# Later gates and additions behind the last scores, and an undivided last output projection, in a gated cross-attention block

## The chip, the cores and the metric

The kernel runs on 1 core of one Trainium2 chip. The metric is the device time of one execution in microseconds (us). The core has engines that run side by side, each through its own instructions in order: TensorE (PE in the profile, with its weight loads as PEld), VectorE (DVE), ScalarE (ACT), GpSimd (POOL) and SyncE (SP), which here issues the transfers. An engine waits for another by a semaphore: the instruction that needs a value waits until the counter has reached it, and everything behind it on that engine waits too.

## The reference

The block is a gated cross-attention followed by a gated mixture layer (4 batches, 256 rows, width 512, context of 1601 rows, 32 query heads over 8 key-value heads of 128):

```python
x = x + tanh(g_xattn) * attention(layernorm(x), ctx)      # q, k, v with biases, softmax, @ Wo + bo
# attention, for each head:
scores = q @ k.T / sqrt(128);  attn = softmax(scores);  o = attn @ v      # v holds the bias bkv
x = x + tanh(g_ffn) * ffn(layernorm(x))
# ffn:
base = h @ base_W.T
w = weights of the two likeliest of 8 experts, softmax(h @ router_W.T)
out = base + 2 * ((h @ lora_A) * w) @ lora_B
```

All of it is float32. For precision most products are made of three: each operand is cut into an upper and a lower part (names that end in `h` and `l`), and the lines of `three` multiply low by high, high by high and high by low.

## The kernel before

**Units and slots.** The attention is cut into 64 units (`UN`; a batch and two heads, 512 columns of q), and each unit into 13 score tiles of up to 128 context rows (`NT`), so there are 832 tiles (`TN`). All engines walk through the same list of slots `s`. In slot `s` TensorE makes the scores of tile `s` into `psS` (two banks, by turns); ScalarE copies them to `xs`; VectorE keeps a running maximum `mrun`. When a unit is done, job `m` turns the maximum, job `b` spreads it over the lanes (`mb` on ScalarE), GpSimd takes it off the scores (L798). In slot `s` ScalarE makes the two exponentials of tile `s - 17` (L988 to `psP`, two banks, for most tiles; L991 to `ph`, a ring of four), VectorE makes the lower part `pl` (L1046) and adds the tile to the unit's sum `psum_` (L1302). The first three tiles of a unit have their sums and lower parts made by GpSimd (L802, L807, and L813, which merges them into the unit before). In slot `s` TensorE multiplies tile `s - 19` by the values (L609 to L611; called PV below, and PV(62, 8) is that of tile 8 of unit 62). The upper part of a tile's exponential may be written only when PV of the tile four before it is done.

**The end of a unit.** Job `s` turns the unit's sum, VectorE reduces it and takes the reciprocal (L1207, L1209), job `r` spreads it (L476), ScalarE copies it to `rbc`, VectorE multiplies the PV result by it (`divide`, L1244), ScalarE makes `oh` with the value bias (L952), VectorE makes `ol` (L1247), and jobs `o0` and `o1` multiply by the output weights (`proj_o`). VectorE adds the product into `acc` (`add_o`, L1085). The last unit, 63, is the last work of the attention.

**The mixture layer.** It runs over 8 row tiles of `x` (0 to 5 from the batches already done, in `x1`; 6 and 7 in `acc`, which need the last unit). `ht` turns the normed tile, `mi` multiplies by the inner weights, the routing on VectorE is four pieces (`route_off`, `route_first`, `route_second`, `route_weights`; the last scales `mid`), `ga` turns the scaled inner tile (L505) for ScalarE to copy (`ffn_gated`), `ya` and `yb` are the two halves of the base product (L519), `yl` adds the last product (`ffn_lora`, L523), and `ffn_out` (L1129) on VectorE adds the result to the tile, after which it is stored. The products of tiles 0 to 5 use the two banks of `psS` by turns, so `ya2` waits until `ffn_out` of tile 0 has run (semaphore `s_yc`), `ya3` for tile 1, and so on.

**What sets the order.** Nothing but the code: a table of names by slot (`names_of` for every unit, and a second table behind it with slots counted from `TN`, the first slot without scores) says which job stands in which slot. TensorE, ScalarE and SyncE act on a job in its slot, VectorE one slot later, behind the running maximum and ahead of the lower part and sum of that slot. PE takes the four banks of `psW` in turn, each when the one that used it before has been read (`take`, `emptied`).

## Time and profile before

| | us |
|---|---|
| median of 3 runs | 2326.78 |
| lowest, highest | 2322.87, 2327.78 |
| the profiled execution | 2328.26 |
| its span in the profile | 2326.4 |
| TensorE busy | 2263.9 (97%) |
| VectorE busy | 1812.9 (78%) |
| ScalarE busy | 1664.8 (72%) |
| GpSimd busy | 1629.7 (70%) |

The profile is one execution; its instructions have a start, a duration and, from the semaphores, the instruction that ended each wait. The last scores are made at 2250 us of the span, and everything that the change touches but two instructions of one column, at slots 26 and 27, lies behind that. A time such as 2277.63 below is a moment of the span in us.

### The profile page before, as it was taken

What the parts mean: (1) busy time and instruction counts of PE and PEld (TensorE: products, weight loads), DVE (VectorE), ACT (ScalarE), POOL (GpSimd) and SP (SyncE); (2) the same over time, 40 slices, a digit from 0 to 9 for tenths busy, and PEclk for the clock granted to TensorE, in tenths of its full rate; (3) what the DMA queues carried; (4) which work ended last, traced back from release to release, by engine and by line L of the source; (5) the groups of instructions that cost most, each with busy time, mean ns of one, the idle gap of its engine ahead of it and who ended that gap; (6) DMA issues with size and microseconds to landing.
All of it is one profiled execution on the core that took longest, in us unless ns stands there. A gap on an engine that the chain in (4) does not pass through costs nothing.

```text
span 2326.4 us, 37328 instructions
## 1 busy us (share of the span) xinstructions
PE 2263.9 (97%) x12333; PEld 1942.2 (83%) x12333; DVE 1812.9 (78%) x3162; ACT 1664.8 (72%) x3149; POOL 1629.7 (70%) x1372
## 2 busy tenths in 40 slices
PE   6999999999999999999999999999999999999998
PEld 6888888888878888888888888888788888888865
DVE  5888888888777787777778778787777778778675
ACT  4777777777767777776777777777777777777663
POOL 5887887967657777856757777875766756766762
PEclk9999999999999999999999999999999999999989
DMA  7344344554333342325214343333423223222211
GB/s 257 132 153 136 128 149 135 159 198 141 98 104 123 112 145 91 125 98 184 91 60 151 97 136 123 110 113 105 168 78 100 91 70 108 64 96 82 87 51 55
DMA packets 139583, 273.69 MB, mean 118 GB/s; under 512 B 22785, under 2 KB 56065, under 8 KB 139137
## 3 DMA queue, kind: packets, MB, share of 16 engines
q1 hardware_dynamic: 122400, 255.71, 32.5%
q10 hardware_dynamic: 16992, 15.59, 2.9%
q8 instruction: 100, 1.64, 0.3%
q14 instruction: 91, 0.74, 0.1%
HBM read 204.27 MB, written 66.98 MB: 117 GB/s over the span
## 4 chain that ended last, share of the span: by engine, by line
PE 77%; DVE 10%; issue 4%; ACT 3%; POOL 3%; DMA 3%; ACTq 0%; DVEq 0%; SPq 0%; POOLq 0%
PE psW L412 11%; PE psW L413 11%; PE psW L414 11%; PE psS L412 6%; PE psS L414 6%; PE psS L413 6%; PE psW L609 6%; PE psW L611 6%; PE psW L610 6%; DVE psum_ L1302 3%; PE psW L468 3%; DVE mrun L1267 3%; POOL xs L798 2%; DMA rbc<-scr_r 1%; PE psW L476 1%
## 5 line engine op out<-in xcount | busy, mean ns | idle before, releaser
L798 POOL TENSOR_TENSOR xs<-xs,mb 128x512 f32<-128x512 f32 (+1 forms) x832 | 1064.5, 1305 | 514.6 <-ACT mb L869 514.5
L1267 DVE TENSOR_TENSOR mrun<-psS,mrun 128x512 f32<-128x512 f32 (+1 forms) x704 | 481.6, 684 | 338.2 <-ACT xs L869 337.2
L869 ACT ACTIVATE xs<-psS 128x512 f32<-128x512 f32 (+1 forms) x832 | 496.9, 597 | 241.2 <-PE psS L414 229.5
L1046 DVE TENSOR_TENSOR pl<-psP,ph 128x512 fp32r<-128x512 f32 (+1 forms) x672 | 458.8, 683 | 93.5 <-ACT ph L991 88.3
L991 ACT ACTIVATE ph<-xs 128x512 fp32r<-128x512 f32 (+1 forms) x832 | 518.6, 623 | 0.1
L1302 DVE TENSOR_TENSOR psum_<-psP,psum_ 128x512 f32<-128x512 f32 (+1 forms) x672 | 456.0, 679 | 0.8 <-POOL pl L802 0.8
L988 ACT ACTIVATE psP<-xs 128x512 f32<-128x512 f32 (+1 forms) x672 | 400.9, 597 | 39.5 <-DVE rinv L1209 14.9
L412 PE MATMUL psS<-ql,kh 128*128 128x512 f32 (+1 forms) x832 | 340.7, 409 | 20.1 <-DVE mrun L1267 18.9
L609 PE MATMUL psW<-ph,vh 128*128 128x512 f32 (+1 forms) x832 | 335.5, 403 | 10.4 <-DVE pl L1046 7.5
L611 PE MATMUL psW<-ph,vl 128*128 128x512 f32 (+1 forms) x832 | 329.2, 396 | 0.0
L610 PE MATMUL psW<-pl,vh 128*128 128x512 f32 (+1 forms) x832 | 328.9, 395 | 0.0
L413 PE MATMUL psS<-qh,kh 128*128 128x512 f32 (+1 forms) x832 | 328.8, 395 | 0.0
L414 PE MATMUL psS<-qh,kl 128*128 128x512 f32 (+1 forms) x832 | 328.7, 395 | 0.0
L412 PE MATMUL psW<-wvl,ch 128*128 128x256 f32 (+1 forms) x832 | 239.7, 288 | 0.0
L413 PE MATMUL psW<-wvh,ch 128*128 128x256 f32 (+1 forms) x832 | 234.5, 282 | 0.0
L414 PE MATMUL psW<-wvh,cl 128*128 128x256 f32 (+1 forms) x832 | 233.8, 281 | 0.0
L609 PEld LDWEIGHTS psW<-ph,vh 128*128 128x128 f32 (+1 forms) x832 | 156.7, 188 | 59.7 <-DVE pl L1046 14.0
L611 PEld LDWEIGHTS psW<-ph,vl 128*128 128x128 f32 (+1 forms) x832 | 156.8, 188 | 37.7
L412 PEld LDWEIGHTS psS<-ql,kh 128*128 128x128 f32 (+1 forms) x832 | 154.5, 186 | 40.3 <-ACT xs L869 16.7
L610 PEld LDWEIGHTS psW<-pl,vh 128*128 128x128 f32 (+1 forms) x832 | 157.4, 189 | 36.3 <-issue 1.9
L414 PEld LDWEIGHTS psS<-qh,kl 128*128 128x128 f32 (+1 forms) x832 | 153.4, 184 | 39.0 <-issue 0.6
L412 PE MATMUL psW<-cl,wkh 128*128 128x384 f32 (+1 forms) x512 | 178.1, 348 | 4.4 <-DVE cl L1046 4.4
(188 smaller groups left out, 4396.5 us busy)
## 6 DMA issues: line engine op xcount, KB each, us to landing
wqh<-scr_wq SPq DMA_DIRECT2D x96, 256.0 KB, 2.6
wql<-scr_wq SPq DMA_DIRECT2D x96, 256.0 KB, 3.0
woh<-scr_wo SPq DMA_DIRECT2D x48, 512.0 KB, 3.2
wol<-scr_wo SPq DMA_DIRECT2D x48, 512.0 KB, 4.2
rbc<-scr_r ACTq DMA_DIRECT2D x59, 256.0 KB, 3.4
scr_wq<-wqh SPq DMA_DIRECT2D x32, 256.0 KB, 2.3
scr_wq<-wql SPq DMA_DIRECT2D x32, 256.0 KB, 2.8
scr_wo<-woh SPq DMA_DIRECT2D x16, 512.0 KB, 3.4
```

The source lines that it names most:

```text
L412: eng.matmul(o, lh, rl, start=first, stop=False)
L413: eng.matmul(o, lh, rh, start=False, stop=False)
L414: return eng.matmul(o, ll, rh, start=False, stop=last)
L609: eng.matmul(o, vh[0:rows, t, hs], hi, start=t == 0, stop=False)
L610: eng.matmul(o, vh[0:rows, t, hs], lo, start=False, stop=False)
L611: eng.matmul(o, vl[0:rows, t, hs], hi, start=False, stop=t == NT - 1).then_inc(s_pv)
L798: eng.tensor_tensor(tile, tile, mb[0:rows_of(t), U % 2, :], ALU.subtract).then_inc(s_sub)
L869: return eng.activation(hi, src, ACT.Copy)
L991: eng.activation(ph[0:rows, T % RP, :], xs[0:rows, T % RX, :], ACT.Exp).then_inc(s_h)
L1046: return eng.tensor_tensor(lo, src, f32(hi), ALU.subtract)
L1267: eng.tensor_tensor(run, psS[0:rows, s % 2, :], a, ALU.max).then_inc(s_m)
L1302: eng.tensor_tensor(total, p, total, ALU.add).then_inc(s_a)
```

## The change

There are two parts.

**The table of the last slots.** The gates `ga0` to `ga5` move from slots 1 to 3 behind the last scores to slots 5 to 8; `yl0` and `yl1` stand together in slot 6, `ya1` and `yb1` come up to slots 2 and 3, and `yb3`, `yl3` and `ya4` move to slot 22. The second half of the routing and the scaling of `mid` (`route_second`, `route_weights`) move on VectorE from the end of slot `TN - 1` and the front of slot `TN` to the end of slot `TN + 3`. A new rule `goes_later` puts `ffn_out` and the additions of unit 62 two slots behind their product, at the end of the slot on VectorE, instead of one slot behind it and ahead of that slot's sums.

**The last unit.** Unit 63 is not divided. ScalarE takes the upper part straight from the PV result, VectorE the lower part, with no value bias. The value bias's own product (`c`, `proj_bias`) is made of a two-part cut of the bias (`bvh`, `bvl`, cut once at slots 26 and 27) times the output weights, 6 products. The four head-and-row-tile products stand apart (`proj_o_apart`), two in `psP` and two in `psW`. VectorE then adds the bias product to both tiles of `acc` (times tanh of the gate), and each of the four products times the reciprocal sums and the gate (`rtg`): 6 additions where there were 2. The turn of the reciprocal (`r`), its copy, and the division are gone, and job `s` of unit 63 stands one slot earlier, ahead of PV(63, 12).

```diff
 
-        return 9 if sum_by_mem(V) else 8
+        return 9 if sum_by_mem(V) else 8 if V < UN - 1 else 6
 
...
         names_of = {0: "k1 - k2 v0 q0 k3 q1 v1 - v2 - v3 -", UN: "- - - - - s - r - - o0 - o1",
-                    UN + 1: "- - - - - s - r - - o0 o1",
+                    UN + 1: "- - - - s c o0 o1",
                     UN - 1: "m - b - p1 s - r - - o0 - -"}.get(U, (AT_MEM if U >= 2 and sum_by_mem(U - 2) else AT)[U % 4])
...
     for s, names in {-15: "ht0", -13: "ht1 mi0", -12: "ht2 mi1", -11: "ht3 mi2", -10: "ht4 mi3", -9: "ht5",
-                     -8: "mi4", -7: "mi5 rt0", -1: "m", 0: "b o ya0", 1: "yb0 ga0 ga1", 2: "yl0 ga2 ga3",
-                     3: "ya1 ga4 ga5", 4: "yb1", 6: "yl1", 8: "ya2", 9: "yb2", 11: "yl2",
-                     14: "ya3", 16: "yb3", 17: "yl3", 21: "ya4"}.items():
+                     -8: "mi4", -7: "mi5 rt0", -1: "m", 0: "b o ya0", 1: "yb0", 2: "ya1", 3: "yb1", 5: "ga0 ga1", 6: "yl0 yl1 ga2 ga3",
+                     8: "ga4 ga5 ya2", 9: "yb2", 11: "yl2", 14: "ya3", 22: "yb3 yl3 ya4"}.items():
         for name in names.split():
...
 
+        def apart(t, h):
+
+            return bank_of(("o", UN - 1, 2 + h)) if t else psP[:, h, :]
+
         def gates_of(i):
...
 
+            def proj_o_apart(t):
+
+                have_weight("o", UN - 1, NU)
+                pe.wait_ge(s_ol, UN)
+                for h in range(2):
+                    if t:
+                        take(("o", UN - 1, 2 + h))
+                    cs = slice(h * 256 + t * 128, h * 256 + (t + 1) * 128)
+                    three(apart(t, h), oh[:, cs], ol[:, cs], woh[:, h, :], wol[:, h, :]).then_inc(s_o)
+                    if t:
+                        emptied(("o", UN - 1, 2 + h), s_acd, 2 * UN + 2 * t + h + 1)
+
+            def proj_bias():
+
+                have_weight("o", UN - 1, NU)
+                pe.wait_ge(s_bvl, 1)
+                o = take(("c", UN - 1, 0))
+                for h in range(2):
+                    m = three(o, bvh[:, 0:1].to_broadcast([128, 128]), bvl[:, 0:1].to_broadcast([128, 128]),
+                              woh[:, h, :], wol[:, h, :], h == 0, h == 1)
+                m.then_inc(s_vb)
+                emptied(("c", UN - 1, 0), s_acd, 2 * UN)
+
             def ffn_mid(i):
...
                     emptied(("pv", s // NT - 2, 0), s_ol, s // NT - 1)
-                if s == TN + 1:
+                if s == TN + 5:
                     emptied(("rt", 0, 0), s_wt, 6)
...
                 u = V % NU
-                act.wait_ge(s_on, V + 1)
+                if V == UN - 1:
+                    act.wait_ge(s_pv, NT * UN)
+                else:
+                    act.wait_ge(s_on, V + 1)
                 if V:
                     act.wait_ge(s_o, 2 * V)
+                if V == UN - 1:
+                    upper(oh[:, :], bank_of(("pv", V, 0))).then_inc(s_oh)
+                    return
                 eng.activation(oh[:, :], bank_of(("pv", V, 0)), ACT.Identity, bias=bkv_sb[:, 8 + u // 2:9 + u // 2]).then_inc(s_oh)
...
                     root(2, 2, NQ)
+                if s == 26:
+                    upper(bvh[:, :], bkv_sb[:, 15:16]).then_inc(s_bvh)
                 if s == NT * (UN - 7) - 1:
...
 
+                if V == UN - 1:
+                    if step == 0:
+                        dve.wait_ge(s_oh, UN)
+                        lower(ol[:, :], bank_of(("pv", V, 0)), oh[:, :]).then_inc(s_ol)
+                    return
                 if step == 0:
...
 
+            def goes_later(kind, n, part):
+
+                return kind == "yl" or kind == "o" and n == UN - 2
+
             def running_max(s):
...
                 for j in jobs.get(s - 1, []):
-                    if (j[0] not in "ms" or not TN - NT < s <= TN) and not goes_first(*j):
+                    if (j[0] not in "ms" or not TN - NT < s <= TN) and not goes_first(*j) and not goes_later(*j):
                         after_job(*j)
-                if s == TN:
-                    route_weights(1)
                 T = s - EXP
...
                         eng.tensor_tensor(total, pair_of(UT)[:, 0, :], total, ALU.add).then_inc(s_a)
+                for j in jobs.get(s - 2, []):
+                    if goes_later(*j):
+                        after_job(*j)
                 if TN - NT <= s < TN:
...
                     floored_var(2, NQ)
+                if s == 27:
+                    dve.wait_ge(s_bvh, 1)
+                    lower(bvl[:, :], bkv_sb[:, 15:16], bvh[:, :]).then_inc(s_bvl)
                 if s == 26:
...
                     route_first(1)
-                if s == TN - 1:
+                if s == TN + 3:
                     route_second(1)
-            add_o(UN - 1, 0)
-            dve.wait_ge(s_acd, 2 * UN - 1)
-            stats(6, tile_of(6))
-            add_o(UN - 1, 1)
-            dve.wait_ge(s_acd, 2 * UN)
-            stats(7, tile_of(7))
+                    route_weights(1)
+            dve.wait_ge(s_r, UN)
+            settle(eng.tensor_scalar(rtg[:, :], rinv[:, (UN - 1) % 2, :], tg[:, 0:1], None, ALU.mult))
+            dve.wait_ge(s_vb, 1)
+            for t in range(2):
+                dve.wait_ge(s_acd, 2 * UN - 2)
+                eng.scalar_tensor_tensor(acc[:, t, :], bank_of(("c", UN - 1, 0)), tg[:, 0:1], acc[:, t, :],
+                                         ALU.mult, ALU.add).then_inc(s_acd)
+            for t in range(2):
+                for h in range(2):
+                    dve.wait_ge(s_o, 2 * UN - 2 + 2 * t + h + 1)
+                    dve.wait_ge(s_acd, 2 * UN - 1 + t if h == 0 else 2 * UN + 2 * t + 1)
+                    eng.scalar_tensor_tensor(acc[:, t, :], apart(t, h), rtg[:, 2 * h + t:2 * h + t + 1], acc[:, t, :],
+                                             ALU.mult, ALU.add).then_inc(s_acd)
+                dve.wait_ge(s_acd, 2 * UN + 2 * t + 2)
+                stats(6 + t, tile_of(6 + t))
             floored_var(6, 8)```

Where its instructions stand. The order is fixed when the program is built. Names are those of the buffers; `[waits ...]` are the semaphores.

TensorE, from the first base product behind the last scores to the base product of tile 2, `ya2` (the row that waits for `s_yc`; left out are most rows of the PVs and of the base products, and repeats). Before, the gates (`mid`) of tiles 0 and 1 stand first of all and the reciprocal (`rinv`) last:

```order
L505 MATMUL psW<-ident,mid 128x128 [waits s_mb,s_wt]
L505 MATMUL psW<-ident,mid 128x128 [waits s_acd,s_wt]
...
L523 MATMUL psS<-lb_sb,midT 128x512 [waits s_gc]
L505 MATMUL psW<-ident,mid 128x128 [waits s_wt]
...
L505 MATMUL psW<-ident,mid 128x128 [waits s_gc] x2
...
L468 MATMUL psW<-ident,psum_ 128x128 [waits s_gc,s_ap]
...
L523 MATMUL psS<-lb_sb,midT 128x512
...
L476 MATMUL psW<-ident,rinv 128x128 [waits s_gc,s_r]
...
L609 MATMUL psW<-ph,vh 128x512 [waits s_lp]
...
L519 MATMUL psS<-bw_sb,hT 128x512 [waits s_yc]
```

```order
L477 MATMUL psW<-ident,psum_ 128x128 [waits s_mb,s_ap]
...
L537 MATMUL psW<-ident,mid 128x128 [waits s_acd,s_wt]
L537 MATMUL psW<-ident,mid 128x128 [waits s_wt]
L645 MATMUL psW<-ph,vh 128x512 [waits s_lp,s_r]
...
L555 MATMUL psS<-lb_sb,midT 128x512 [waits s_gc] x2
L537 MATMUL psW<-ident,mid 128x128 x2
...
L485 MATMUL psW<-ident,rinv 128x128 [waits s_gc]
...
L537 MATMUL psW<-ident,mid 128x128 [waits s_gc]
L537 MATMUL psW<-ident,mid 128x128 [waits s_rb]
L551 MATMUL psS<-bw_sb,hT 128x512 [waits s_yc]
```

The turn of the sum of unit 62 (`psum_`) now stands ahead of all gates, PV(63, 0) waits for the reciprocal (`s_r`), and both first `yl` stand together behind it.

VectorE, from the reciprocal of unit 62 to its `ol` (`x<-psS` is `ffn_out`; the first `pl` is that of tile 3 of unit 63, the second that of tile 4):

```order
L1209 RECIPROCAL rinv<-ssum 128x4 [waits s_d]
L1129 SCALAR_TENSOR_TENSOR x<-psS,tg,x 128x512 [waits s_y]
L1046 TENSOR_TENSOR pl<-psP,ph 128x512 [waits s_h]
L1302 TENSOR_TENSOR psum_<-psP,psum_ 128x512 [waits s_lp]
L1244 TENSOR_TENSOR psW<-psW,rbc 128x512 [waits s_rb,s_pv]
L1046 TENSOR_TENSOR pl<-psP,ph 128x512 [waits s_h]
L1302 TENSOR_TENSOR psum_<-psP,psum_ 128x512 [waits s_a]
L1247 SCALAR_TENSOR_TENSOR ol<-psW,bkv_sb,oh 128x512 [waits s_oh]
```

```order
L1253 RECIPROCAL rinv<-ssum 128x4 [waits s_d]
L1090 TENSOR_TENSOR pl<-psP,ph 128x512 [waits s_h]
L1353 TENSOR_TENSOR psum_<-psP,psum_ 128x512 [waits s_lp]
L1293 TENSOR_TENSOR psW<-psW,rbc 128x512 [waits s_rb,s_pv]
L1090 TENSOR_TENSOR pl<-psP,ph 128x512 [waits s_h]
L1353 TENSOR_TENSOR psum_<-psP,psum_ 128x512 [waits s_a]
L1173 SCALAR_TENSOR_TENSOR x<-psS,tg,x 128x512 [waits s_y] x2
L1296 SCALAR_TENSOR_TENSOR ol<-psW,bkv_sb,oh 128x512 [waits s_oh]
```

Before, `ffn_out` of tile 0 stood four rows above the first row shown, and that of tile 1 is the second row here; now both stand behind tile 4 of unit 63.

VectorE at the end, from the last unit's sum to its last statistics:

```order
L1207 TENSOR_REDUCE ssum<-psW 128x4 [waits s_rt,s_su]
L1209 RECIPROCAL rinv<-ssum 128x4 [waits s_d]
L1244 TENSOR_TENSOR psW<-psW,rbc 128x512 [waits s_rb,s_pv]
L1247 SCALAR_TENSOR_TENSOR ol<-psW,bkv_sb,oh 128x512 [waits s_oh]
L1085 SCALAR_TENSOR_TENSOR acc<-psW,tg,acc 128x512 [waits s_acd,s_o]
L1090 BN_STATS steps<-acc 128x6 [waits s_acd]
L1092 BN_AGGR mv<-steps 128x2 [waits s_bs]
L1085 SCALAR_TENSOR_TENSOR acc<-psW,tg,acc 128x512 [waits s_o,s_d]
L1090 BN_STATS steps<-acc 128x6 [waits s_acd]
```

```order
L1253 RECIPROCAL rinv<-ssum 128x4 [waits s_d]
L1090 TENSOR_TENSOR ol<-psW,oh 128x512 [waits s_oh]
L1173 SCALAR_TENSOR_TENSOR x<-psS,tg,x 128x512 [waits s_y]
L1401 TENSOR_SCALAR rtg<-rinv,tg 128x4 [waits s_r]
L1405 SCALAR_TENSOR_TENSOR acc<-psW,tg,acc 128x512 [waits s_acd,s_vb,s_d]
L1405 SCALAR_TENSOR_TENSOR acc<-psW,tg,acc 128x512
L1411 SCALAR_TENSOR_TENSOR acc<-psP,rtg,acc 128x512 [waits s_acd,s_o] x2
L1134 BN_STATS steps<-acc 128x6 [waits s_acd]
L1136 BN_AGGR mv<-steps 128x2 [waits s_bs]
L1411 SCALAR_TENSOR_TENSOR acc<-psW,rtg,acc 128x512 [waits s_o,s_d]
L1411 SCALAR_TENSOR_TENSOR acc<-psW,rtg,acc 128x512 [waits s_acd,s_o]
L1134 BN_STATS steps<-acc 128x6 [waits s_acd]
```

`ffn_out` of tile 3 (`x<-psS`) now stands between the last `ol` and the six additions.

## Rows read from the trace of the kernel before

**Rows 1.** The page: the span, TensorE's busy time, and the chain that ended last.

```profile
span 2326.4 us, 37328 instructions
...
PE 2263.9 (97%) x12333; PEld 1942.2 (83%) x12333; DVE 1812.9 (78%) x3162; ACT 1664.8 (72%) x3149; POOL 1629.7 (70%) x1372
...
PE 77%; DVE 10%; issue 4%; ACT 3%; POOL 3%; DMA 3%; ACTq 0%; DVEq 0%; SPq 0%; POOLq 0%
```

**Rows 2.** Stretches behind the last scores: length, busy by engine, granted clock, DMA.

```profile
2250.40:2257.00 6.60, 4.08 (x17) 2.92 (x16) 6.23 (x14) 3.31 (x7) 1.30 (x2) 0.76 0.00 0
2257.00:2261.00 4.00, 4.00 (x10) 2.64 (x10) 3.73 (x16) 1.63 (x3) 3.15 (x3) 0.54 0.11 18
2261.00:2271.00 10.00, 10.00 (x36) 5.76 (x34) 5.15 (x9) 5.17 (x14) 6.04 (x6) 1.00 0.25 98
...
2301.20:2312.00 10.80, 10.74 (x36) 6.12 (x36) 5.92 (x16) 1.07 (x3) 0.00 (x0) 1.00 0.07 25
```

**Rows 3.** ScalarE's timeline: start, duration, line, tiles; in brackets the wait.

```profile
2258.19 0.62 ACT L991 ACTIVATE ph<-xs 128x512 fp32r<-128x512 f32 x1
...
2264.52 0.45 ACT L869 ACTIVATE midT<-psW 128x128 f32<-128x128 f32 x2 [5.71 <-PE psW L505]
...
2272.88 0.62 ACT L991 ACTIVATE ph<-xs 128x512 fp32r<-128x512 f32 x1
```

**Rows 4.** VectorE's timeline behind the last scores.

```profile
2256.30 0.21 DVE L1163 TENSOR_TENSOR psW<-psW,rs 128x48 f32<-128x48 f32 x1
...
2258.65 1.27 DVE L1178 TENSOR_TENSOR mid<-mid,psW 128x128 f32<-128x128 f32 x6
...
2267.24 0.74 DVE L1129 SCALAR_TENSOR_TENSOR x<-psS,tg,x 128x512 f32<-128x512 f32 x1
...
2272.58 0.69 DVE L1207 TENSOR_REDUCE ssum<-psW 128x4 f32<-128x512 f32 x1 [3.37 <-PE psW L468]
```

**Rows 5.** GpSimd's timeline: the merge of unit 62's sum.

```profile
2269.29 1.28 POOL L813 TENSOR_TENSOR psum_<-pp,psum_ 128x512 f32<-128x512 f32 x1 [3.96 <-DVE psum_ L1302]
```

**Rows 6.** TensorE's timeline: behind the last scores, and at the last unit's end.

```profile
2262.49 1.88 PE L519 MATMUL psS<-bw_sb,hT 128*128 128x512 f32 x4
...
2274.37 0.50 PE L609 MATMUL psW<-ph,vh 128*128 128x512 f32 x1 [0.27 <-POOL pl L802]
...
2276.83 0.50 PE L609 MATMUL psW<-ph,vh 128*128 128x512 f32 x1 [1.06 <-POOL pl L802]
...
2277.63 1.88 PE L519 MATMUL psS<-bw_sb,hT 128*128 128x512 f32 x4
...
2297.50 0.65 PE L476 MATMUL psW<-ident,rinv 128*128 128x128 f32 x4 [1.00 <-DVE rinv L1209]
...
2301.20 0.47 PE L412 MATMUL psW<-wol,oh 128*128 128x512 f32 x1 [1.32 <-issue]
...
2310.05 1.02 PE L523 MATMUL psS<-lb_sb,cst 128*128 128x512 f32 x2
2310.91 0.60 PE L468 MATMUL psW<-ident,hn 128*128 128x128 f32 x4
```

**Rows 7.** VectorE's timeline at the end.

```profile
2302.86 0.75 DVE L1085 SCALAR_TENSOR_TENSOR acc<-psW,tg,acc 128x512 f32<-128x512 f32 x1 [1.76 <-PE psW L414]
...
2305.37 0.69 DVE L1090 BATCH_NORM_STATS2 steps<-acc 128x6 f32<-128x512 f32 x1
...
2307.75 0.55 DVE L1120 TENSOR_SCALAR hn<-acc,mv,rstd 128x512 f32<-128x512 f32 x1
```

**Rows 8.** TensorE's timeline around another fall of the clock.

```profile
1094.71 0.47 PE L412 MATMUL psS<-ql,kh 128*128 128x512 f32 x1 [1.77 <-DVE mrun L1267]
...
1096.51 0.62 PE L609 MATMUL psW<-ph,vh 128*128 128x512 f32 x1 [0.86 <-DVE pl L1046]
```

**Rows 9.** Stretches behind that, columns as in rows 2.

```profile
1096.70:1100.10 3.40, 3.40 (x11) 2.51 (x11) 3.40 (x7) 2.93 (x7) 3.40 (x4) 0.51 0.01 4
1100.10:1103.50 3.40, 3.40 (x19) 2.72 (x18) 3.40 (x8) 2.28 (x5) 0.43 (x1) 0.99 0.02 5
```

More of the change, by code:

```diff
@@ L90, in gated_block @@
                 n = {"m": U - 1, "b": U - 1, "s": U - 2, "r": U - 2, "o": U - 2, "p": U - 3, "q": U + 1, "v": U // 4,
-                     "k": (U + 1) // 2, "x": U // NU + 1, "-": -1}[kind]
-                top = {"m": UN, "b": UN, "s": UN, "r": UN, "o": UN, "p": MEM_SUM, "q": UN, "v": 4 * B, "k": NK, "x": B, "-": 0}[kind]
+                     "c": U - 2, "k": (U + 1) // 2, "x": U // NU + 1, "-": -1}[kind]
+                top = {"m": UN, "b": UN, "s": UN, "r": UN, "o": UN, "c": UN, "p": MEM_SUM, "q": UN, "v": 4 * B, "k": NK, "x": B, "-": 0}[kind]
                 if not 0 <= n < top or (kind == "x" and U % NU < 14):
@@ L212, in gated_block @@
         rinv = sb("rinv", [128, 2, 4], F32)
+        rtg = sb("rtg", [128, 4], F32)
+        bvh = sb("bvh", [128, 1], F32R)
+        bvl = sb("bvl", [128, 1], F32R)
         steps = sb("steps", [128, 40], F32)
@@ L260, in gated_block @@
         s_o = sem("s_o")
+        s_vb = sem("s_vb")
         s_ht = sem("s_ht")
@@ L278, in gated_block @@
         s_ex = sem("s_ex")
+        s_bvh = sem("s_bvh")
         s_m = sem("s_m")
@@ L309, in gated_block @@
         s_dx = sem("s_dx")
+        s_bvl = sem("s_bvl")
         s_wt = sem("s_wt")
@@ L533, in job @@
                     proj_q(n, part)
+                elif kind == "o" and n == UN - 1:
+                    proj_o_apart(part)
+                elif kind == "c":
+                    proj_bias()
                 elif kind == "o":
```

## The prediction

> **What bounds the kernel now.** I read the page first. TensorE is busy in 97% of the span and carries 77% of the chain that ended last [rows 1], so a step elsewhere counts only where TensorE waits for it. Everything that the change moves lies behind the last scores at 2250 us, so I then read that stretch by windows. The granted clock is 0.76 in a window of 6.6 us and 0.54 in the next 4.0, so it stood at its lower level, 1.2 GHz, for 0.24 x 2 x 6.6 + 0.46 x 2 x 4.0 = 6.9 us, and from 2261 to 2271 TensorE is busy for 10.00 of 10.00 us at the full clock [rows 2]. Next the timelines. ScalarE waits 5.71 us for the first two gates, with exponentials queued behind them [rows 3]. That delays the last sums of unit 62 on VectorE, and GpSimd's merge waits 3.96 us for these [rows 5]. What of this reaches TensorE is little: 0.27 and 1.06 us ahead of PV(63, 1) and PV(63, 2), then 1.00 us ahead of `r` and 1.32 us ahead of the last `o0` [rows 6]. Together 3.65 us. From 2301.20 on it is busy again: 10.74 of 10.80 us [rows 2].
>
> So the ceiling of this change is 3.65 us plus the `r` that is dropped, 0.45 us (0.65 recorded, of which 0.2 is the overlap with what follows), and it adds six products of 512 columns. Ten such pieces of work fill 4.00 us at 0.54 of the clock [rows 2], 0.4 each, and about 0.23 at the full clock (a group of four base products, 1.88 us from 2277.63 with an overlap of 0.16, is 1.72, so 0.43 for a product that takes two passes more) [rows 6]. The bias product costs 6 x 0.23 = 1.39 us. The most to be had is 3.65 + 0.45 - 1.39 = 2.7 us, 0.12%.
>
> **The gates, step by step.** The times to PV(62, 8) at 2261.40 stay as they are, since nothing on its chain moves.
>
> 1. ScalarE no longer waits for the gates. The exponentials of tiles 11 and 12 of unit 62 run from 2258.7 (behind the one that starts at 2258.19 [rows 3]) and from 2261.7, and the last ends at 2263.3: its `ph` has to wait for PV(62, 8). VectorE adds tile 12 by 2264.6 instead of 2269.2. The routing pieces that stood ahead of it, from 2256.30 to the start of the six `mid` products at 2258.65 and 1.2 us of these, together 3.54 us [rows 4], now run behind it, from 2264.6 to 2268.1. GpSimd merges at 2265.3, when it is through with its subtractions, instead of 2269.29 [rows 5]. So far 4 us are won, off TensorE.
> 2. TensorE from 2262.49 [rows 6]: three pairs of base products (1.72 each) and four PVs (0.70 each) to 2270.4, the turn of the sum (0.45), then `ga0` and `ga1` (0.35) to 2271.2. It has no wait there, as it had none before.
> 3. PV(63, 0) takes the bank of the turned sum, so it waits for the reduction and the reciprocal. The reduction takes 0.69 us [rows 4], the reciprocal 0.2, from 2271.05: TensorE goes on at 2272.0, a new wait of 0.75 us.
> 4. PV(63, 0), `yl0`, `yl1`, `ga2`, `ga3` take 0.77 + 1.72 + 0.35: to 2274.8. On ScalarE the exponentials of tile 3 of unit 63 stand behind the copies of `ga2` and `ga3`. They end at 2276.4 where they ended at 2273.5 before [rows 3].
> 5. VectorE takes them in its order: tile 3 (2 x 0.60) to 2277.65, the division of unit 62 (0.60, its input is there at 2276.95), tile 4 (1.2) to 2279.45, and only then `ffn_out` of tile 0, recorded at 0.74 us [rows 4]: it ends at 2280.2. Before, this ran at 2267.24, ten microseconds ahead of its need.
> 6. TensorE is through PV(63, 1), `r`, PV(63, 2), `ga4` and `ga5` at 2277.3. `ya2` needs the bank that `ffn_out` of tile 0 reads, and waits until 2280.2: **2.9 us**, a wait that was not there. Everything else of TensorE is queued behind it. `ya2` started at 2277.63 before [rows 6]. It is now 2.5 us late.
>
> **The last unit.** From `ya2` to `ht6` TensorE took 2310.91 - 2277.63 = 33.28 us [rows 6]. Out go the two waits, 2.32 us, and `r`, 0.45. In comes the bias product, 1.39, which covers ScalarE's `oh` and VectorE's `ol` but for 0.2 us. All other jobs are the same, in another order. Moving `yb3`, `yl3` and `ya4` behind `o1` has a second effect. `ffn_out` of tile 3 is ahead of the six additions on VectorE and waits for `yl3`, so the additions don't run beside `o0` and `o1`. From the end of `yl3`: 7 operations of 0.75 (the duration of an addition [rows 7]), 0.2 for `rtg`, 0.95 for the first statistics, then the old chain from the second statistics at 2305.37 to `hn` at 2307.75, 2.38, and 0.55 for `hn` itself [rows 7]: 5.25 + 0.2 + 0.95 + 2.38 + 0.55 = 9.3. TensorE has two tiles' products behind `yl3`, 2 x 4.3 = 8.6 us (the last 0.86 of it from 2310.05 to 2310.91 [rows 6]). The difference, with the lag of the first end, is a wait of some 0.85 us ahead of `ht6`. Before, `hn` had been done 2.6 us before TensorE came to it. The stretch is then 33.28 - 2.32 - 0.45 + 1.39 + 0.2 + 0.85 = 32.95 us, 0.33 less. From `ht6` on nothing changes.
>
> Sum without the clock: 2.5 - 0.3 = **+2.2 us**.
>
> **Costs that no row shows.** The cut of the bias is one column on ScalarE and on VectorE, in a stage where TensorE bounds; a like small operation took 0.21 us [rows 4]. Between nothing and 0.4 us; I take nothing. A product into `psP` and one from a broadcast column have no row; the nearest are those of `o0`, and I take these, between -0.1 and +0.3 us in all.
>
> **The clock.** Around 1094 TensorE waited 1.77 and 0.86 us with one set of scores between [rows 8], and then ran at 0.51: 11 pieces in 3.40 us, where the next 3.40 us at 0.99 had 19 [rows 9]. At 0.43 a product of 512 columns instead of 0.23, 3.4 us at the low level cost 3.4 x (1 - 0.23/0.43) = 1.6 us. Behind the last scores such a fall lasted twice as long, about 3.2 us lost by the same count, less what waits lie in it [rows 2]. A wait of 2.9 us is longer than both of these together, and TensorE is fully fed behind it, so I count one fall to 1.2 GHz for 3.4 us: **+1.6 us**. With it the forecast is 2.2 + 1.6 = 3.8 us. The Trainium skill (TensorE: Matmul & The Clock Gate, "Why this matters for your kernels") names idle gaps of more than about 3 us between bursts as what takes the clock down; by that 2.9 us would cost nothing beyond themselves. The trace speaks against it, with a fall behind 1.77 and 0.86 us.
>
> **The forecast.** The profiled execution took 2328.26 us, 1.5 more than the median of the runs, and its span was 2326.4. On its scale the changed kernel takes 2328.3 + 3.8 = 2332.1, and as a median 2326.8 + 3.8 = **2330.6 us**, 0.16% more. A measurement can tell about 0.2% from no change here, 4.65 us.
>
> **The rivals.**
>
> - *No fall of the clock* (the skill's rule, or a wait cut in two by a small piece of work). For it: waits of 1.00 and 1.32 us near 2300 cost no clock. Against it: rows 8. It gives +2.2: 2329.0. Chance 0.15.
> - *Slower: the fall lasts twice as long.* If the clock falls while TensorE still waits for `ffn_out`, the rest of the wait lies in the low stretch, and the low level goes on for 6.9 us as it did behind the last scores [rows 2]. The point from which it decides is whether the clock falls while a good part of the wait is still to come, or behind it. Price 3.2 less what of the wait lies in it, so 2.8: +5.0, 2331.8. Chance 0.27.
> - *The gain comes through.* If `ffn_out` of tile 0 were done when TensorE is through with `ga5` at 2277.3, no new wait is left, the four old ones go, and the result is -2.7: 2324.1. For it: GpSimd and the sums of unit 62 are 4 us earlier. Against it: VectorE's order is fixed, and the exponentials that stand ahead come behind `ga3`. Chance 0.07.
> - *My forecast*, 0.45. The rest, 0.06, is for what I haven't seen.
>
> **How the numbers follow.** Faster by over 0.2% needs more than the whole of the old waits: 0.04. Slower by over 0.2% is the second rival, and a tenth of the forecast: 0.34. Within 0.2%: 0.62. The range takes in the first three cases, leaves out the gain, and allows for the runs of before lying up to 3.9 us under their median: 2326.5 to 2333.0.
>
> **What would show it.** In the profile of the changed kernel: GpSimd's merge 4 us earlier behind the last scores; ScalarE's wait for the first gates short; a wait of 2.9 us on TensorE ahead of `ya2`, released by VectorE's `ffn_out`; VectorE waiting 5 us or more for `yl3` ahead of the additions; a wait of 0.5 to 1.2 us ahead of `ht6`; one stretch at 0.5 of the clock behind the long wait. I am wrong if `ya2` starts without a wait (then the gain comes through), if the clock stays at 1 behind it, or if the stretch from `ya2` to `ht6` is longer than 35 us, which would mean that the products in `psP` or the six additions cost more than the rows say.

## The result, and the profile after

| | before | after |
|---|---|---|
| median | 2326.95 us (2322.20 to 2329.09, 20 runs) | 2329.74 us (2327.38 to 2331.78, 20 runs) |
| ratio, after to before | | 1.0015, 95% interval 1.0009 to 1.0022 |
| profiled execution | 2328.26 us, span 2326.4 | 2328.24 us, span 2326.4 |

The changed kernel is slower by 2.8 us between the medians, and by 3.5 us (2.1 to 5.1) by the ratio. The forecast was 2330.6, 3.8 us more.

The page says next to nothing of this. These are its lines that answer to [rows 1]:

```profile
span 2326.4 us, 37336 instructions
...
PE 2263.0 (97%) x12335; PEld 1938.0 (83%) x12335; DVE 1815.4 (78%) x3167; ACT 1662.0 (71%) x3149; POOL 1633.0 (70%) x1372
...
PE 75%; DVE 11%; issue 4%; POOL 4%; ACT 4%; DMA 3%; ACTq 0%; DVEq 0%; SPq 0%; POOLq 0%
```

The span is that of before, to 0.1 us, in a kernel that is 3 us slower. The reason is what comes ahead of the changed part. It is the same work in every kernel of this study, yet the last scores were reached anywhere from 2247.1 to 2255.2 us in the 14 profiles, and all 14 hold stretches at 1.2 GHz ahead of them, in varying number and place. So I compare what follows. **The tail** is the time from the start of the last product of the last scores (2250.37 before, 2248.11 after) to the end of the span: 2326.4 - 2250.4 = 76.0 us before and 78.25 after. Even this needs care, since the profile of before has a fall of the clock in its tail [rows 2] that most of the other profiles lack, as will be seen. (A fall is a stretch in which the granted clock is at 1.2 GHz instead of 2.4.)

These places of the changed kernel's timelines carry the reading. First TensorE behind the last scores (start, duration, line, tiles; in brackets the wait), to be held against [rows 6]:

```profile
2248.11 0.39 PE L423 MATMUL psS<-qh,kl 128*65 128x512 f32 x1
...
2266.97 0.50 PE L645 MATMUL psW<-ph,vh 128*128 128x512 f32 x1 [0.78 <-DVE rinv L1253]
...
2275.11 3.78 PE L551 MATMUL psS<-bw_sb,hT 128*128 128x512 f32 x4 [2.96 <-DVE x L1173]
2277.90 1.42 PE L645 MATMUL psW<-ph,vh 128*128 128x512 f32 x1
...
2310.84 0.66 PE L477 MATMUL psW<-ident,hn 128*128 128x128 f32 x4 [0.90 <-DVE hn L1164]
```

The four old waits are gone, and three new ones stand here: 0.78 us ahead of PV(63, 0), 2.96 us ahead of `ya2`, 0.90 us ahead of `ht6`. The long one ends with VectorE's `x`, which is `ffn_out`. VectorE's timeline shows what kept that:

```profile
2271.31 0.69 DVE L1090 TENSOR_TENSOR pl<-psP,ph 128x512 fp32r<-128x512 f32 x1 [4.40 <-ACT ph L1033]
2271.92 0.68 DVE L1353 TENSOR_TENSOR psum_<-psP,psum_ 128x512 f32<-128x512 f32 x1
2272.51 0.69 DVE L1293 TENSOR_TENSOR psW<-psW,rbc 128x512 f32<-128x512 f32 x1
2273.11 0.68 DVE L1090 TENSOR_TENSOR pl<-psP,ph 128x512 fp32r<-128x512 f32 x1
2273.71 0.68 DVE L1353 TENSOR_TENSOR psum_<-psP,psum_ 128x512 f32<-128x512 f32 x1
2274.31 1.40 DVE L1173 SCALAR_TENSOR_TENSOR x<-psS,tg,x 128x512 f32<-128x512 f32 x2
```

VectorE first stands still for 4.40 us, for exponentials that are queued behind `ga3` on ScalarE, then does tile 3, the division and tile 4, and then `ffn_out`. Its input had been there since the two `yl` products ended at about 2269.6, during the 4.40 us in which VectorE had nothing to do.

GpSimd's merge, to be held against [rows 5], has lost its wait:

```profile
2262.22 1.27 POOL L849 TENSOR_TENSOR psum_<-pp,psum_ 128x512 f32<-128x512 f32 x1
```

The windows across the long wait and behind it (length, busy time by engine, granted clock):

```profile
2272.15:2275.10 2.95, 0.00 (x0) 0.00 (x0) 2.95 (x6) 2.84 (x8) 2.95 (x4) 0.84 0.00 0
2275.10:2278.50 3.40, 3.39 (x5) 1.51 (x5) 3.40 (x6) 1.50 (x3) 2.14 (x2) 0.50 0.00 0
2278.50:2281.00 2.50, 2.50 (x6) 1.51 (x5) 0.39 (x2) 0.80 (x2) 0.00 (x0) 0.50 0.00 0
2281.00:2284.40 3.40, 3.40 (x14) 2.31 (x13) 1.80 (x4) 1.45 (x3) 0.00 (x0) 1.00 0.00 0
```

TensorE did nothing in the first. The clock fell to 1.2 GHz in its last microsecond (0.84 granted, so 0.16 x 2 x 2.95 = 0.9 us) and stayed there for 5.9 us more, in which TensorE got through 5 and 6 pieces of work where it then did 14 in 3.40.

### The profile page after: what moved, and what is told of

Read it like the earlier page. It is cut to its first block, busy times and chain, and to the rows that moved or that the text cites. A ratio compares the mean times of both kernels' runs of the same rounds, so it can differ in the third digit from the quotient of the medians.

```text
span 2326.4 us, 37336 instructions
## 1 busy us (share of the span) xinstructions
PE 2263.0 (97%) x12335; PEld 1938.0 (83%) x12335; DVE 1815.4 (78%) x3167; ACT 1662.0 (71%) x3149; POOL 1633.0 (70%) x1372
## 4 chain that ended last, share of the span: by engine, by line
PE 75%; DVE 11%; issue 4%; POOL 4%; ACT 4%; DMA 3%; ACTq 0%; DVEq 0%; SPq 0%; POOLq 0%
PE psW L421 11%; PE psW L423 11%; PE psW L422 11%; PE psS L421 6%; PE psS L423 6%; PE psS L422 6%; PE psW L645 6%; PE psW L647 6%; PE psW L646 6%; DVE psum_ L1353 3%; DVE mrun L1320 3%; PE psW L477 3%; POOL xs L834 2%; DVE pl L1090 1%; DMA rbc<-scr_r 1%
## 5 line engine op out<-in xcount | busy, mean ns | idle before, releaser
L1320 DVE TENSOR_TENSOR mrun<-psS,mrun 128x512 f32<-128x512 f32 (+1 forms) x704 | 482.2, 685 | 337.1 <-ACT xs L905 336.0
L1090 DVE TENSOR_TENSOR pl<-psP,ph 128x512 fp32r<-128x512 f32 (+1 forms) x672 | 459.4, 684 | 96.7 <-ACT ph L1033 91.8
L1033 ACT ACTIVATE ph<-xs 128x512 fp32r<-128x512 f32 (+1 forms) x832 | 518.7, 623 | 8.2 <-PE psW L647 8.2
L1353 DVE TENSOR_TENSOR psum_<-psP,psum_ 128x512 f32<-128x512 f32 (+1 forms) x672 | 456.9, 680 | 0.9 <-POOL pl L838 0.9
L421 PE MATMUL psS<-ql,kh 128*128 128x512 f32 (+1 forms) x832 | 340.6, 409 | 20.0 <-DVE mrun L1320 18.8
L645 PE MATMUL psW<-ph,vh 128*128 128x512 f32 (+1 forms) x832 | 335.7, 404 | 9.6 <-DVE pl L1090 7.2
L423 PE MATMUL psS<-qh,kl 128*128 128x512 f32 (+1 forms) x832 | 329.0, 395 | 0.0
L646 PE MATMUL psW<-pl,vh 128*128 128x512 f32 (+1 forms) x832 | 328.3, 395 | 0.0
L421 PE MATMUL psW<-wvl,ch 128*128 128x256 f32 (+1 forms) x832 | 238.9, 287 | 0.0
L423 PE MATMUL psW<-wvh,cl 128*128 128x256 f32 (+1 forms) x832 | 233.8, 281 | 0.0
L645 PEld LDWEIGHTS psW<-ph,vh 128*128 128x128 f32 (+1 forms) x832 | 156.5, 188 | 58.8 <-DVE pl L1090 13.4
L646 PEld LDWEIGHTS psW<-pl,vh 128*128 128x128 f32 (+1 forms) x832 | 157.1, 189 | 37.1 <-issue 2.2
L421 PEld LDWEIGHTS psS<-ql,kh 128*128 128x128 f32 (+1 forms) x832 | 154.4, 186 | 39.6 <-ACT xs L905 16.4
L423 PEld LDWEIGHTS psS<-qh,kl 128*128 128x128 f32 (+1 forms) x832 | 153.4, 184 | 39.4 <-issue 0.2
L421 PE MATMUL psW<-cl,wkh 128*128 128x384 f32 (+1 forms) x512 | 177.8, 347 | 4.2 <-DVE cl L1090 4.2
```

Source lines behind the costliest of these rows:

```text
L421: eng.matmul(o, lh, rl, start=first, stop=False)
L423: return eng.matmul(o, ll, rh, start=False, stop=last)
L645: eng.matmul(o, vh[0:rows, t, hs], hi, start=t == 0, stop=False)
L646: eng.matmul(o, vh[0:rows, t, hs], lo, start=False, stop=False)
L1033: eng.activation(ph[0:rows, T % RP, :], xs[0:rows, T % RX, :], ACT.Exp).then_inc(s_h)
L1090: return eng.tensor_tensor(lo, src, f32(hi), ALU.subtract)
```

## The experiments

My theory was that of the prediction: the long wait comes from `ffn_out`'s new place, the gains ahead of it don't reach TensorE, and the fall of the clock comes from the wait. Twelve runs tell it from its rivals. `fill` issues products of 512 columns from tiles that are there, into a free bank; nobody reads their result. Tails are those of one profile each, and medians those of 11 or 12 runs beside 33 to 35 of before.

| kernel | median, ratio to before (95%) | tail | clock in the tail |
|---|---|---|---|
| e1_out_early | 2325.30, 0.9997 (0.9988 to 1.0006) | 72.8 | full |
| e2_filled_wait | 2328.01, 1.0011 (1.0002 to 1.0019) | 75.1 | full |
| e3_yl3_early | 2330.15, 1.0018 (1.0009 to 1.0026) | 75.4 | 3.4 us low |
| e4_both | 2322.98, 0.9987 (0.9978 to 0.9996) | 72.7 | 3.4 us low |
| e5_table_only | 2327.75, 1.0006 (0.9996 to 1.0015) | 77.1 | 6.8 us low |
| e6_last_unit_only | 2325.73, 0.9996 (0.9985 to 1.0006) | 72.1 | full |
| e8_filled_m | 2326.02, 0.9993 (0.9984 to 1.0002) | 73.5 | full |
| e9_both_filled_m | 2325.18, 0.9997 (0.9987 to 1.0007) | 71.1 | full |
| e10_both_yb1 | 2320.57, 0.9979 (0.9969 to 0.9989) | 70.1 | full |
| e11_change_again | 2329.22, 1.0013 (1.0004 to 1.0022) | 77.0 | 3.4 us low |
| e12_filled_again | 2327.09, 1.0005 (0.9997 to 1.0014) | 75.3 | full |
| e13_both_again | 2324.75, 0.9992 (0.9984 to 1.0001) | 71.0 | full |

("Clock in the tail" leaves out what lies at the very end of the execution, from 70 us behind the last scores on.) Before's median was 2325.92 beside e1 to e4, 2326.24 beside e5 to e9, and 2325.78 beside e10 to e13.

### The place of `ffn_out` makes the wait: e1_out_early

```diff
-                return kind == "yl" or kind == "o" and n == UN - 2
+                return kind == "yl" and n >= 2 or kind == "o" and n == UN - 2
```

> The changed kernel with one thing undone: ffn_out of tiles 0 and 1 stands again one slot behind its product on VectorE, ahead of the sums of tiles 3 and 4 of unit 63. Theory (the long wait is VectorE's order): the wait of 2.96 us ahead of ya2 shrinks under 0.5 us, the clock does not fall behind it, and the sum against before is +2.2 - 2.9 = -0.7 us: 2326.2 us, a ratio of 0.9997 to before, 3.5 us under the changed kernel. Rival (the loss is in the last unit, its bias product and six additions; the long wait only moves a later one): it stays at 2329 to 2330 us, 1.001.

VectorE's timeline, at the place shown above, and TensorE's (the gate's turn, and `ya2` right behind it):

```profile
2271.87 1.61 DVE L1173 SCALAR_TENSOR_TENSOR x<-psS,tg,x 128x512 f32<-128x512 f32 x2 [1.92 <-PE psS L555]
```

```profile
2274.59 0.61 PE L537 MATMUL psW<-ident,mid 128*128 128x128 f32 x2
2275.03 1.88 PE L551 MATMUL psS<-bw_sb,hT 128*128 128x512 f32 x4
```

`ffn_out` now runs in VectorE's idle time, `ya2` starts without a wait, and the clock stays full. The tail is 4.2 us shorter than that of e11, which is the change itself run once more. The only price is a new wait of 0.46 us ahead of the turn of the sum of unit 63. The median is level with before. So what makes the changed kernel slower than before is the wait of 2.96 us and its fall, and both come from this one rule.

### The fall comes from the wait: e2_filled_wait, e11_change_again, e12_filled_again

The first and the third are the same edit, eight products ahead of `ya2`; the second is the changed kernel once more, beside it on the same chip.

```diff
                 elif kind == "ya":
+                    if n == 2:
+                        fill(8)
                     ffn_base(n, 0)
```

> The changed kernel with eight products of 512 columns, whose result nobody reads, ahead of ya2 on TensorE, in the bank that the next output product takes. They lie inside the wait, so the wait's end stays, only TensorE is not idle. Theory (the wait brings a fall of the clock that costs by itself): the granted clock stays at 1 behind ya2, ya2 starts at the same distance from the last scores, and the median falls by 1.6 to 2.5 us to 2327.2 to 2328.1. Rival (the clock falls but nothing hangs on it, or the fall is owed to the stage before): within 0.5 us of the changed kernel's 2329.7.

> The changed kernel once more, beside the next two on the same chip. Expected 2.8 us over before, with a fall of the clock behind the wait of 2.96 us.

> e2_filled_wait once more, beside the changed kernel. Theory (the fall costs by itself): 1.6 to 2.5 us under e11_change_again, and no fall behind ya2. Rival: within 0.5 us of it.

The same three stretches of e11: the wait, and 3.4 us behind it twice:

```profile
2274.20:2277.20 3.00, 0.05 (x1) 0.05 (x1) 3.00 (x6) 2.90 (x8) 3.00 (x4) 1.00 0.00 0
2277.20:2280.60 3.40, 3.40 (x5) 1.40 (x6) 3.40 (x6) 1.45 (x3) 2.07 (x2) 0.54 0.00 0
2280.60:2284.00 3.40, 3.40 (x12) 2.09 (x11) 1.49 (x3) 1.15 (x3) 0.00 (x0) 0.96 0.00 0
```

And of e12, with its products on TensorE's timeline:

```profile
2271.15:2274.10 2.95, 2.08 (x8) 1.43 (x8) 2.95 (x6) 2.85 (x8) 2.95 (x4) 1.00 0.00 0
2274.10:2277.50 3.40, 3.40 (x11) 1.83 (x11) 3.40 (x6) 1.75 (x4) 2.14 (x2) 1.00 0.00 0
```

```profile
2272.02 2.11 PE L431 MATMUL psW<-kh 128*128 128x512 f32 x8 [0.87 <-ACT cst L915]
2274.11 1.99 PE L559 MATMUL psS<-bw_sb,hT 128*128 128x512 f32 x4
```

`ya2` starts no earlier: 2274.11 - 2247.10 = 27.0 us behind the last scores in e12, 2277.15 - 2250.18 = 27.0 in e11. But with the wait filled, all but 0.87 us at its start, the clock stays full. The tails are 77.0 and 75.3, and the medians, on one chip, 2329.22 and 2327.09. A fall of 3.4 us costs 1.7 us by the tails. The medians say 2.1, roughly: single executions of either kernel lie up to 7 or 8 us apart, and falls of both lengths go into them. Another pair gives the same price: e4 and e13 are one kernel, with and without a fall of 3.4 us in the tail, and their tails are 72.7 and 71.0. In the profile after the low stretch is 6.8 us, and its tail is 78.25 - 75.3 = 2.9 us over the filled one. The long wait came with a fall in all four profiles that have it (after, e3, e5, e11), and in neither of the two with it filled.

The traces hold more such waits, ahead of the last scores. In nine of the 14 profiles TensorE waits 2.72 to 2.77 us near 2207 us for the running maximum, and in e10 it waits 3.18 us near 538. All ten came with a fall, which began 2.0 us behind the wait's end at the latest. In the other five profiles the wait near 2207 is 1.51 to 1.74 us, with one of 0.87 close behind, and these have a fall there too. This is the place in the profile after (TensorE's timeline), whose clock fell at 2209.3:

```profile
2207.32 0.47 PE L421 MATMUL psS<-ql,kh 128*128 128x512 f32 x1 [2.76 <-DVE mrun L1320]
...
2209.13 0.67 PE L645 MATMUL psW<-ph,vh 128*128 128x512 f32 x1 [0.86 <-DVE pl L1090]
```

### The late `yl3`: e3_yl3_early, e4_both, e13_both_again

```diff
-                     8: "ga4 ga5 ya2", 9: "yb2", 11: "yl2", 14: "ya3", 22: "yb3 yl3 ya4"}.items():
+                     8: "ga4 ga5 ya2", 9: "yb2", 11: "yl2", 14: "ya3", 16: "yb3", 17: "yl3", 21: "ya4"}.items():
```

e4 and e13 have this edit and that of e1.

> The changed kernel with yb3, yl3 and ya4 in their old slots 16, 17 and 21, so that ffn_out of tile 3 has run before the six additions are due. Theory (the additions are late because they stand behind yl3): the wait of 0.90 us ahead of ht6 is gone and the time falls by 0.9 us to 2328.8. Rival (the additions themselves bound): the wait stays between 0.5 and 1 us, and the time at 2329.7.

> Both: ffn_out of tiles 0 and 1 early and yb3, yl3, ya4 in their old slots. Theory: both waits and the fall are gone, against before -0.7 - 0.9 = -1.6 us or a little more, 2325.3, ratio 0.9993. Rival (what is taken off TensorE here comes back as another wait of the last unit, as ahead of the sum's turn or of the first output product): no better than e1_out_early, 2326.2 or more.

> e4_both once more, beside the changed kernel. Theory: 2 us under before and 4.5 to 5 us under e11_change_again. Rival (its first ratio of 0.9987 was luck in where the clock fell elsewhere): within 1 us of before.

In e3 the turn of `hn` has no bracket any more (TensorE's timeline):

```profile
2313.07 0.60 PE L477 MATMUL psW<-ident,hn 128*128 128x128 f32 x4
```

The tail, with the long wait and a fall of 3.4 us still in it, is 1.7 us shorter than that of e11. Not all of this is the wait of 0.90 us. Some 0.3 is the first wait behind the last scores, 0.84 us here and 1.15 in e11, and some 0.3 is the fall's place: it began 26.1 us behind the last scores, with 0.5 us of the wait left, and behind the wait in e11. Its median shows no gain at all. That one is a miss, and I can't tell it from the medians' scatter. The pair with `ffn_out` early in both shows it better. From e1 to e4, on one chip, the median falls from 2325.30 to 2322.98 us, and from e1 to e13 the tail falls by 1.8, with the waits of 0.46 and 0.90 us both gone. Against the change as a whole, with `ffn_out` early as well, the order is clear: 2322.98 and 2324.75 us, where the changed kernel had 2329.22 beside the latter. From e13 to e12, both with the full clock throughout, the tail grows by 75.3 - 71.0 = 4.3 us: 2.96 + 0.90 of waits, and 0.4 that I can't place.

### The two halves: e5_table_only, e6_last_unit_only

e5 is the kernel before with the new table, `goes_later` and the routing's new place, and the last unit divided as before. e6 is the kernel before with the last unit's change alone. Their diffs are the two parts of the one shown ahead.

> The kernel of before with the table of the last slots, goes_later and the later routing of the change, and the old divided last unit. Theory: the wait ahead of ya2 (2.9 us) and the fall behind it are all there, and yb3, yl3, ya4 in slot 22 cover the last unit's wait of 1.32 us: +2.5 - 1.3 = +1.2 us without the clock, 2.8 to 3.7 with the fall: about 2330. Rival (the loss is in the undivided last unit): 2326 to 2327.

> The kernel of before with the undivided last unit alone, all jobs of the mixture layer in their old slots. Theory: the waits of 1.00 and 1.32 us and the turn of the reciprocal, 0.45, go, the bias product, 1.39, and 0.2 us ahead of the first output product come: -1.2 us, 2325.8, ratio 0.9995, and no wait ahead of ht6. Rival (the undivided unit costs more than it saves): 2328 or more.

TensorE's timeline of e5, at `ya2`, and then that of e6, which has no bracket between the two lines shown, where the waits of 1.00 and 1.32 us had been:

```profile
2274.95 3.78 PE L518 MATMUL psS<-bw_sb,hT 128*128 128x512 f32 x4 [2.95 <-DVE x L1128]
```

```profile
2272.85 0.50 PE L646 MATMUL psW<-ph,vh 128*128 128x512 f32 x1 [1.05 <-POOL pl L839]
...
2306.66 2.12 PE L531 MATMUL psW<-la_sb,hT 128*128 128x136 f32 x16 [0.25 <-ACT hT L906]
```

The harm is the table's: e5 has the long wait and the fall, with a tail of 77.1. This rests on the tail. The median is only 1.5 us over that of before, where 2330 had been expected, and the ratio's interval takes in 1. The last unit's change is a gain by its tail: 72.1, 1.4 us under the 73.5 of e8, which is before with the full clock (its median, 0.5 us under before, can't be told from none). The halves don't add up. The wait of 1.32 us goes in either, so it counts once; the wait of 0.90 us is there only when `yl3` is late and six additions follow it. e5 less its fall (2.9) is 0.7 over e8, so 0.7 - 1.4 + 1.3 + 0.9 = 1.5, where e12 lies 75.3 - 73.5 = 1.8 over e8.

### The fall right behind the last scores: e8_filled_m, e9_both_filled_m

e8 is the kernel before, e9 is e4, both with five products ahead of the turn of the maximum of unit 63 and five behind it.

```diff
                 elif kind == "m":
+                    if n == UN - 1:
+                        fill(5)
                     pe.wait_ge(s_m, 12 * (n + 1))
                     turn(("m", n, 0), mrun[:, n % 2, :], s_mt, s_nm, n + 1)
+                    if n == UN - 1:
+                        fill(5)
```

> The kernel of before with five products of 512 columns that nobody reads ahead of the last job m and five behind it, in the bank that the next job takes, so that TensorE is busy in the two waits of 1.14 and 1.38 us behind the last scores. Theory (these waits bring the fall of the clock that the profile of before shows from 2254 to 2261): the granted clock stays at 1 there, the stretch from PV(62, 7) to the second base product shrinks from 7.85 to about 5.0 us, and the median falls by up to 2.8 us, less where a run had no such fall: 2324 to 2326. Rival (the products only delay the two jobs, or the fall is owed to something else): 2327 or more.

> e4_both with the products of e8_filled_m as well. Theory: the two gains add up, -1.6 and -1 to -2.8: 2322.5 to 2324.5, faster than before and than the changed kernel. Rival (e4_both without the fall gains nothing from the filling, since its time is set elsewhere): as e4_both.

The window of e8 that answers to the first two of [rows 2]:

```profile
2252.70:2262.00 9.30, 9.26 (x40) 6.53 (x39) 8.00 (x25) 4.84 (x10) 2.92 (x3) 1.00 0.15 49
```

The clock is full, the tail 2.5 us shorter than in the profile of before, and the median 0.2 us under that of before, with a ratio whose interval takes in 1: no gain can be told, where up to 2.8 us had been expected. The two agree once one counts the profiles. Twelve of the 14 leave this place unfilled, with waits of 0.8 to 1.2 us and 1.38 us with one piece of work between, and only two of them (before, e4) have the fall. So I had read a rare event as part of the kernel. e9 gives nothing over e4 either. Its tail (71.1) is that of e13 (71.0), which is the same kernel without the products, so filling a wait costs nothing by itself, and e8 can stand for before at the full clock, to some 0.2 us: up to `ya2`, e6 is before with these waits unfilled and the clock full, and there `ya2` starts 2273.66 - 2248.78 = 24.9 us behind the last scores, and in e8 2277.36 - 2252.66 = 24.7.

### A version that beats both: e10_both_yb1

e4, with `yb1` behind the turn of the sum of unit 62, where it covers the reduction and the reciprocal for which PV(63, 0) waits:

```diff
-0: "b o ya0", 1: "yb0", 2: "ya1", 3: "yb1", 5: "ga0 ga1",
+0: "b o ya0", 1: "yb0", 2: "ya1", 5: "yb1 ga0 ga1",
```

> e4_both with yb1 moved from slot 3 to slot 5, behind the turn of unit 62's sum and ahead of ga0, so that its 1.72 us lie over the reduction and the reciprocal for which PV(63, 0) waits 0.78 us. Theory: that wait goes, and the tail from the last scores shrinks by 0.8 us against e4_both (to about 70.3 us without a fall of the clock behind the last scores); ratio 0.998 to 0.9985. Rival (the turn of the sum, now reached 1.7 us earlier, waits for GpSimd's merge instead): a new wait of about that size ahead of it and no gain.

```profile
2270.70 0.60 PE L477 MATMUL psW<-ident,psum_ 128*128 128x128 f32 x4
2271.13 1.88 PE L551 MATMUL psS<-bw_sb,hT 128*128 128x512 f32 x4
...
2272.99 0.48 PE L645 MATMUL psW<-ph,vh 128*128 128x512 f32 x1
```

```profile
2255.20:2325.20 70.00, 63.93 (x230) 38.31 (x228) 50.33 (x113) 29.11 (x58) 23.82 (x20) 1.00 0.18 60
```

The wait of 0.78 us is gone (TensorE's timeline), and the whole tail runs at the full clock (the window). The tail is 0.9 us shorter than that of e13. The median is 4.2 us under e13's and 5.2 us under before's, 0.9979 (0.9969 to 0.9989). Of the 5.2 us the tail explains 73.5 - 70.1 = 3.4; the rest must lie ahead of the last scores, where the kernels are alike, and stays open.

## Why the prediction held, step by step

**The gates.** GpSimd merges without a wait, 2262.22 - 2248.11 = 14.1 us behind the last scores; 2265.3 - 2250.4 = 14.9 had been expected, with before's fall of the clock in it. Against before that is 4.8 us by the profile of before, but only 2.3 by that of e8, which has no fall:

```profile
2269.03 1.28 POOL L825 TENSOR_TENSOR psum_<-pp,psum_ 128x512 f32<-128x512 f32 x1 [2.47 <-DVE psum_ L1314]
```

Part of what I had seen as the gates' harm was the fall's. None of the gain reaches TensorE either way. One sign came out less plainly than it was put: ScalarE still waits 3.02 us for the first gates, where a short wait had been expected and 5.71 was before. But no exponential of unit 62 is queued behind it any more. On TensorE, the wait for the reciprocal is 0.78 us (0.75 expected), the long wait 2.96 (2.9), released by `ffn_out` as said. Against before with the full clock, `ya2` starts 27.0 - 24.7 = 2.3 us late by e8, and 2.1 by e6; 2.5 were expected.

**The last unit.** VectorE waited 5.71 us for `yl3` (5 or more expected), and the chain behind it, first addition to the end of `hn`, is as counted:

```profile
2301.39 0.75 DVE L1173 SCALAR_TENSOR_TENSOR x<-psS,tg,x 128x512 f32<-128x512 f32 x1 [5.71 <-PE psS L555]
...
2302.31 1.41 DVE L1405 SCALAR_TENSOR_TENSOR acc<-psW,tg,acc 128x512 f32<-128x512 f32 x2
2303.64 1.59 DVE L1411 SCALAR_TENSOR_TENSOR acc<-psP,rtg,acc 128x512 f32<-128x512 f32 x2
...
2310.24 0.55 DVE L1164 TENSOR_SCALAR hn<-acc,mv,rstd 128x512 f32<-128x512 f32 x1
```

From 2301.39 to 2310.79 are 9.4 us, 9.3 were expected, and 0.90 us of wait for 0.85. From `ya2` to `ht6` e12, whose clock is full, took 2306.94 - 2274.11 = 32.83 us; 32.95 were expected, 33.28 was before. A product into `psP` and one from a broadcast column cost no more than the nearest rows said, to 0.1 us in all: in the profile after, the six of the bias start 0.23 us apart (2294.16 to 2295.33), and the six into `psP` 0.25 (2295.74 to 2297.00).

One stated sign of being wrong did come up. In the profile after, `ya2` to `ht6` is 2310.84 - 2275.11 = 35.73 us, over the limit of 35, which was to mean dear products or additions. It means neither here. The stretch is 2.9 us longer than in e12, whose clock is full, and the products and additions cost what was forecast. The surplus is the long fall, which the limit had not allowed for; in e11, with the short one, the stretch is 34.6.

**The sum without the clock** is then 2.3 - 0.5 = +1.8 us (75.3 - 73.5 by the tails; 1.6 by e6's place of `ya2`), for +2.2.

**The clock.** One fall of 3.4 us was priced at 1.6 us. It cost 1.7 in e11. The second rival was the fall of twice that length, priced at 2.8; after had it, and it cost 2.9. So the profiled execution followed the rival, not the forecast. The rival's point of decision, whether the clock falls while a good part of the wait is still to come, fits: 6.8 us where about 1 us of the wait was left when the clock fell (after, and e5), 3.4 where 0.5 or nothing was left (e3, e11). The falls near 2210 us divide in the same way. In the five profiles in which that one lasted 6.8 us, TensorE waited for 0.5 to 0.8 us more behind the moment of the fall, and in the nine with 3.4 us for 0.3 or less. No run sets that moment, so it isn't shown. Which one is the usual can't be read from two profiles of one kernel. By the tails they make +3.5 and +4.8 us against before at the full clock; the ratio gives 3.5 (2.1 to 5.1), which leans to the forecast.

The rule of the Trainium skill (TensorE: Matmul & The Clock Gate, "Why this matters for your kernels"), that gaps above about 3 us take the clock down, would have given +2.2. These runs disagree with it, and the measurement decides. The wait of 2.96 us is near the rule's bound, but it came with a fall in four of four, waits of 2.72 to 2.77 us in nine of nine, and [rows 8] has a fall behind 1.77 and 0.86. For waits as short as those of [rows 8], though, the argument was weaker than it looked. Here is the same place in the profile after, the waits and the window over them:

```profile
1093.63 0.47 PE L421 MATMUL psS<-ql,kh 128*128 128x512 f32 x1 [1.47 <-DVE mrun L1320]
...
1095.43 0.50 PE L645 MATMUL psW<-ph,vh 128*128 128x512 f32 x1 [0.87 <-DVE pl L1090]
```

```profile
1093.60:1100.40 6.80, 4.74 (x20) 3.09 (x21) 5.99 (x11) 6.45 (x14) 5.83 (x5) 1.00 0.33 119
```

Waits little shorter, and no fall. Of the 14 profiles 8 have one there. The first wait is not the same in all: it is 1.39 to 2.14 us in the eight with a fall and 0.79 to 1.84 in the six without; of the eight waits of 1.5 us or more seven were followed by one. So shorter waits make a fall possible, and near 2207 us those of 1.51 to 1.74 with 0.87 behind them had one in five of five. Waits of 2.7 us and more brought it wherever they stand, 14 of 14 with the four of 2.96.

**What was mis-sized** is the start of the scale. The profile of before had a fall in the stretch that I compared with, worth 76.0 - 73.5 = 2.5 us, and I took its execution as 1.5 us over the median for that and all else. That the sum came out within a microsecond of the ratio owes something to errors on either side: the terms without the clock are 0.4 us less than written, and the fall cost 1.7 us in one profile of the changed kernel and 2.9 in the other, for 1.6.

**The gain comes through**, the third rival, has its answer too. Its condition, `ffn_out` done before TensorE wants the bank, is e1's edit, and the gain is then not 2.7 us but 73.5 - 72.8 = 0.7 by the tails. Its price was summed wrongly. It left out the waits of 0.75 and 0.85 us that the prediction itself had put ahead of PV(63, 0) and `ht6`; with them it would have been 2.7 - 0.75 - 0.85 = 1.1. With the late `yl3` undone as well, e13's tail is 2.4 us under e8's, and the medians of e4 and e13 are 2322.98 and 2324.75, where 2324.1 had been worked out. Another sum of the prediction doesn't add up either: the second rival and a tenth of the forecast are 0.27 + 0.045 = 0.315, not 0.34.

## What to carry to other kernels

Work that is put off on an in-order engine, because its result isn't needed for long, still holds the bank it reads: look at who waits for that bank, and at what stands between on the engine's queue. When a change gives TensorE a wait like this one of 2.96 us, add the price of a fall of the clock, and remember that harmless products in the wait took that price away in both runs that had them. And where a profile of before holds a fall of the clock in the very stretch that a change touches, see whether others have it there before taking it for part of the kernel.
